# Attention maxima split on DVE before their transposition, copied out by ScalarE, and the output product moved ahead of it

## What is computed

```
q, k = rope(q), rope(k)                      # q = layernorm(x), k = v = context
Q, K, V = q @ Wq.T + bq, k @ Wk.T + bk, v @ Wv.T + bv      # 16 heads of 8
attn = softmax(Q K^T / sqrt(8)); out = (attn V) @ Wo.T + bo
x = x + tanh(g_xattn) * out
x = x + tanh(g_ffn) * ffn(layernorm(x))      # 8 experts of 352, top 2 of a router
```

## Time and profile before

| | us |
|---|---|
| median of 3 runs | 434.19 |
| lowest, highest | 433.54, 435.53 |
| the profiled execution, its own time | 435.61 |
| its span, first to last instruction | 433.8 |

### The profile page before, as it was taken

How to read it: one execution, slowest core, us unless ns; L and a number is a source line. 1 busy time by engine, 2 the same in 40 slices (tenths; PEclk the granted TensorE clock), 3 DMA queues, 4 the chain that set the end, 5 groups by cost and what they waited for, 6 DMA issues and landing times.

```text
span 433.8 us, 13431 instructions
## 1 busy us (share of the span) xinstructions
PE 391.3 (90%) x3876; PEld 267.6 (62%) x3877; DVE 302.5 (70%) x1167; ACT 260.1 (60%) x582; POOL 244.8 (56%) x201
## 2 busy tenths in 40 slices
PE   8997888999889888988998899998999999999991
PEld 3445454565656545555655578686777878778771
DVE  5878878898898978979786565568655555555550
ACT  3518577786967768676756665644455555454540
POOL 7073233135665555745343367888887458876663
PEclk9999999999999999999998999999999999999997
DMA  7525152353867914325101324544454334444320
GB/s 198 157 60 137 28 133 67 88 145 108 223 162 206 217 55 111 102 58 132 52 29 47 98 59 78 92 65 98 78 76 59 50 48 57 62 52 57 34 24 0
DMA packets 57423, 39.08 MB, mean 90 GB/s; under 512 B 8819, under 2 KB 55158, under 8 KB 57366
## 3 DMA queue, kind: packets, MB, share of 16 engines
q1 hardware_dynamic: 43622, 28.87, 26.1%
q0 software_dynamic: 12736, 8.64, 14.2%
q10 hardware_dynamic: 1008, 0.85, 0.8%
HBM read 14.26 MB, written 11.75 MB: 60 GB/s over the span
## 4 chain that ended last, share of the span: by engine, by line
PE 50%; DVE 17%; DMA 11%; issue 7%; SPq 6%; ACT 4%; POOLq 2%; POOL 1%; DVEq 0%; ACTq 0%
PE bank L1614 9%; PE bank L1592 7%; PE bank L1594 7%; DMA out<-ys,yi 5%; DVE nmx L847 5%; DMA ks<-parts 4%; PE bank L1604 4%; SPq L249 4%; PE bank L1374 3%; PE bank L1401 2%; PE bank L1348 2%; SPq L282 2%; PE bank L1316 2%; PE bank L1317 2%; ACT pt L580 2%
## 5 line engine op out<-in xcount | busy, mean ns | idle before, releaser
L516 POOL DMA_INDIRECT out<-ys,yi x72 | 111.8, 1553 | 43.5 <-issue 23.0
L427 POOL DMA_INDIRECT slots_dram<-xr,slu x64 | 65.5, 1024 | 75.0 <-ACT onT L593 55.1
L847 DVE TENSOR_REDUCE nmx<-bank 128x4 f32<-128x512 f32 x128 | 81.7, 680 | 4.3 <-PE bank L1348 4.3
L580 ACT ACTIVATE pt<-bank 128x512 f32<-128x512 f32 x128 | 72.5, 595 | 9.3 <-PE bank L1361 8.2
L1614 PEld LDWEIGHTS bank<-wf_sb,hT 128*128 128x128 f32 (+1 forms) x432 | 56.9, 190 | 22.7 <-issue 18.0
L1200 DVE TENSOR_TENSOR hh<-sg,bank 128x352 f32<-128x352 f32 x72 | 37.4, 520 | 47.9 <-ACT sg L714 27.2
L1614 PE MATMUL bank<-wf_sb,hT 128*128 (+1 forms) x432 | 61.0, 277 | 4.7 <-DVE hT L1210 4.6
L722 ACT ACTIVATE ys<-bank,yc 128x128 f32<-128x128 f32 x72 | 26.5, 368 | 64.0 <-PE bank L1614 60.1
L1592 PE MATMUL bank<-wf_sb,xT 128*128 x144 | 55.2, 465 | 0.1
L1594 PE MATMUL bank<-wf_sb,xT 128*128 x144 | 54.3, 459 | 0.0
L1374 PE MATMUL bank<-pt,v 128*9 128x128 f32 x1024 | 49.4, 276 | 3.7 <-ACT pt L580 2.5
(11 more groups left out here) (193 smaller groups left out, 707.9 us busy)
## 6 DMA issues: line engine op xcount, KB each, us to landing
qs<-parts SPq DMA_DIRECT2D x48, 128.0 KB
ks<-parts SPq DMA_DIRECT2D x45, 128.0 KB
xs<-slots_dram SPq DMA_DIRECT2D x72, 66.0 KB
wf_sb<-in_wup SPq DMA_DIRECT2D x8, 352.0 KB
x_sb<-in_x SPq DMA_DIRECT2D x8, 256.0 KB, 3.7
ctx_sb<-in_ctx_in SPq DMA_DIRECT2D x8, 256.0 KB, 4.5
out<-x_sb SPq DMA_DIRECT2D x8, 256.0 KB, 2.5
out<-ys,yi POOLq DMA_INDIRECT x72, 3.4
```

The source lines that it names most:

```text
L427: nc.gpsimd.indirect_dma_start(out=slots_dram, out_offset=bass.IndirectOffsetOnAxis(ap=slu[:, c % 2, k, kk:kk + 1], axis=0), in_=xr[:, c % ...
L516: nc.gpsimd.indirect_dma_start(out=out.rearrange("b s d -> (b s) d"), out_offset=bass.IndirectOffsetOnAxis(ap=yi[:, r:r + 1], axis=0), in_ ...
L580: nc.scalar.activation(pt[:, 4 * g:4 * g + 4, :], STB[g % 2][:, :].rearrange("p (h s) -> p h s", h=4), ACT.Exp, scale=SCORE_SCALE).then_in ...
L847: nc.vector.tensor_reduce(nmx[:, b % 2, at:at + 4], SB[g % 2][:, :].rearrange("p (h s) -> p h s", h=4), AX.X, ALU.max, negate=True).then_i ...
```

## The change

The maxima are split into two bf16 parts by DVE before the transposition (`split_high`, `split_low`, on 128 queries x 16 heads in SBUF). PE transposes both parts at once, 32 columns, by a bf16 product with the identity. ScalarE copies the result out of PSUM (`maximum_out`), behind `heads_out` of the next iteration. On PE the transposition moves behind `project_out`. SP, PE and POOL wait for the copy (`a_mT`) where they waited for L858. POOL's `low` gets a wait at u = 0 (for `choose_sum` of chunk c - 2) and at u = 3 (for the split of batch b + 2). Before the loop, the first remainder of chunk 1 moves behind the split of batch 1.

```diff
-        mTs = sb("mTs", [NH, 2, NMAX, S], BF16)
+        nm2 = sb("nm2", [128, 2, NMAX, NH], BF16)
+        mTs = sb("mTs", [NMAX * NH, 2, S], BF16)
-        mT_ps = SB[1][0:NH, 0:S]
+        mT_ps = SB[1][0:NMAX * NH, 0:S]
 ...
# SP, maxima
-                sp.wait_ge(d_mT, b + 1)
+                sp.wait_ge(a_mT, b + 1)
-                    sp.dma_start(qs[row:128:64, b // CH % NST, :, t0:t0 + S], mTs[:, b % 2, part, :])\
+                    sp.dma_start(qs[row:128:64, b // CH % NST, :, t0:t0 + S], mTs[NH * part:NH * (part + 1), b % 2, :])\
# POOL, scatter_early
-                pool.wait_ge(d_mT, min(b + 2, B))
+                pool.wait_ge(a_mT, min(b + 2, B))
# POOL, u == 0
                     if there(c + 1):
+                        if there(c - 2):
+                            pool.wait_ge(d_mb, c - 1)
                         low(c + 1, 1)
# POOL, u == 3
                     if there(c + 2):
+                        pool.wait_ge(d_ms, b + 3)
                         low(c + 2, 0)
# ScalarE
+            def maximum_out(b):
+                act.wait_ge(pe_mT, b + 1)
+                if b >= 2:
+                    act.wait_ge(m_in[b % 2], 32 * (b // 2))
+                nc.scalar.activation(mTs[:, b % 2, :], mT_ps, ACT.Copy).then_inc(a_mT, 1)
 ...
             high(1, 1, PR)
+            maximum_out(0)
             middle(1, 0)
+            maximum_out(1)
 ...
                 if real(b - 1):
                     heads_out(b - 1)
+                if b and real(b + 1):
+                    maximum_out(b + 1)
# DVE
-                if g == 0 and b >= 2:
-                    dve.wait_ge(pe_mT, b - 1)
 ...
-            def maximum_high(b):
-                dve.wait_ge(pe_mT, b + 1)
+            def split_high(b):
+                dve.wait_ge(d_max, 4 * b + 4)
                 if b >= 2:
-                    dve.wait_ge(m_in[b % 2], 32 * (b // 2))
-                nc.vector.tensor_copy(mTs[:, b % 2, 0, :], mT_ps).then_inc(d_mh, 1)
-
-            def maximum_low(b):
+                    dve.wait_ge(pe_mT, b - 1)
+                nc.vector.tensor_copy(nm2[:, b % 2, 0, :], nmx[:, b % 2, :]).then_inc(d_mh, 1)
+
+            def split_low(b):
                 dve.wait_ge(d_mh, b + 1)
-                nc.vector.tensor_tensor(mTs[:, b % 2, 1, :], mT_ps, mTs[:, b % 2, 0, :], ALU.subtract).then_inc(d_mT, 1)
+                nc.vector.tensor_tensor(nm2[:, b % 2, 1, :], nmx[:, b % 2, :], nm2[:, b % 2, 0, :], ALU.subtract).then_inc(d_ms, 1)
 ...
-            maximum_high(0)
-            maximum_low(0)
+            split_high(0)
+            split_low(0)
             for g in range(4):
                 maximum(1, g)
+            split_high(1)
+            split_low(1)
             remainder(1, 0, HB)
-            maximum_high(1)
-            maximum_low(1)
             remainder(1, 1, PR)
# PE
                 if g == 1 and b:
-                    pe.wait_ge(d_mT, b)
+                    pe.wait_ge(a_mT, b)
 ...
-                pe.wait_ge(d_max, 4 * b + 4)
-                nc.tensor.transpose(mT_ps, nmx[:, b % 2, :], ident).then_inc(pe_mT, 1)
+                pe.wait_ge(d_ms, b + 1)
+                mm(mT_ps, nm2[:, b % 2, :, :].rearrange("p a h -> p (a h)"), identb, start=True, stop=True).then_inc(pe_mT, 1)
 ...
+                if real(b - 1):
+                    project_out(b - 1)
                 if real(b + 2):
                     transpose_maximum(b + 2)
-                if real(b - 1):
-                    project_out(b - 1)
```

More of the change, by code:

```diff
@@ L193, in flamingo @@
         d_rq, d_rk, p_lq, p_lk, d_mh = map(sem, ("d_rq", "d_rk", "p_lq", "p_lk", "d_mh"))
+        d_ms, a_mT = sem("d_ms"), sem("a_mT")
         stack_in = [sem("stack_in0"), sem("stack_in1")]
@@ L200, in flamingo @@
             sem, ("a_tg", "a_xh", "a_xT", "a_exp", "a_aT", "a_xn", "a_nT", "a_e"))
-        d_max, d_mT, d_rc, d_on, d_x1, d_q = map(sem, ("d_max", "d_mT", "d_rc", "d_on", "d_x1", "d_q"))
+        d_max, d_rc, d_on, d_x1, d_q = map(sem, ("d_max", "d_rc", "d_on", "d_x1", "d_q"))
         d_stat, d_ve, d_rs, d_stat2, d_ve2, d_t2, d_sc2, d_rt, d_top, d_m12, d_slot, d_sl, d_pr = map(
@@ L1155, in _ @@
                 if real(b + 2):
-                    maximum_high(b + 2)
-                    maximum_low(b + 2)
+                    split_high(b + 2)
+                    split_low(b + 2)
                 if u == 1 and there(c + 2):
@@ L1499, in _ @@
                 keep_warm(STB[0], 1)
+            pe.wait_ge(cast, 1)
             transpose_maximum(0)
@@ L1504, in _ @@
             transpose_maximum(1)
-            pe.wait_ge(cast, 1)
             for b in range(B):
```

## The result

The changed kernel took 441.77 to 449.05 us in four runs, median 444.06, against 433.54 to 435.53 for the kernel before on the same chip. The ratio is 1.019 with an interval of 1.0135 to 1.024; on a second chip it was 1.021 (1.015 to 1.026). It is slower by about 2%: 434.19 times 1.019 is 442.4 us.

A forecast was written before the change was run, and what follows sets the result against it. The attention part was taken as paced by a round of all engines ahead of the maxima of u = 0, behind which SP's `ks` transfers stand. Delays over five chunks and the rest sum to 4.5 us: 438.7 us, range 431.5 to 442.5.

The forecast's parts named there:

- the two turns of ScalarE's queue: Turns u = 3 to 0 and 0 to 1: `oT` late behind `base` or `normalise`, copy behind it; 0.4 and 0.45 us.
- The operations: New or changed operations: split 0.19 us each, copy 0.28 with 0.18 of queue, L923 about 0.17, transposition 0.07 less.
- 2 us over 32 batches at most: PE's queue: the bf16 transposition takes about 0.05 us instead of 0.12, 0.07 less per batch.
- The turns: Four batch-to-batch turns of the chunk from 98.04: 0.25, 0.2, 0.4 and 0.45 us late, 1.3 in sum.
- ScalarE gets the copy, behind `heads_out`: ScalarE's queue: the copy starts 0.48 us after `oT` and takes 0.28; the second group of `scores` waits for it.
- 0.2 at u = 2: Turn u = 2 to 3: DVE does four statistics ahead of the split, so PE waits about 0.2 us for it.
- DVE's relief: DVE at u = 0: L923 freed from POOL's `low`, 3.4 us in five chunks; as rival it decides, faster, chance 0.2.
- The rival at 430.2 us: DVE's relief decides: L923's 3.4 us and the saved round trip come through, 4.0 us faster; chance 0.2.
- POOL holds the split: Rival at u = 0: POOL's `low` of k holds the split's subtraction, up to 1.2 us in five chunks, 444.7; chance 0.07.
- The wait costs nothing: POOL at u = 0: `low` of k, waiting for `choose_sum`, is done near 117.7, before SP wants it after 121.4.
- I count 0, with 1.5 us either way: Start, up to 45 us: first split makes maxima 0.1 us later, a `shift` may pass POOL sooner; counted as 0.
- 0.8, 0.6 and 0.1 us: Delays forecast for the chunk from 45.67, the chunk from 125.04 and everything from 180 us on.

The follow-up runs named there:

- the order alone: The output product put ahead of the transposition, nothing else changed, against the kernel before: 1.028 (1.023 to 1.0325).
- the kernel without products: The kernel before without the eight 128x512 products PE does between the first eight groups of scores, against the kernel before: 1.002 (0.998 to 1.006).

## Why the prediction was right, and where it was short

It forecast slower, 438.7 us within 431.5 to 442.5. The ratio makes 442.4, inside by 0.1 us and just outside the forecast's own 436 to 442; the median of the four runs as they stand is 444.06, above both. The change costs 8.2 us where the sum was 4.5. The direction and the two turns of ScalarE's queue were foreseen; that the size fell inside is luck. By its steps:

- **The operations.** Split 0.17 each (predicted 0.19), copy 0.25 with 0.15 of queue (0.28 and 0.18), L923 at 0.17: right. PE's transposition was to hold its queue 0.07 us less and holds it 0.04 more, and the stretch with the output product is 0.15 longer, 4.8 us over the kernel where "2 us over 32 batches at most" were to be won. This has the sign wrong.
- **The turns.** PE waits for the copy behind `oT` at u = 3 to 0 and u = 0 to 1, 0.96 to 0.97 and 0.55 us in each of chunks 2 to 5, and in chunk 1, which has no `base` yet, at u = 0 to 1 alone. For the split it waits 2.7 us in all, three times ahead of the first mark and once at u = 2 (0.54 us at 54.79); at u = 2 of the chunk shown it loses 0.06, and most of the 0.20 is PE's longer stretch. `heads_by_query` stands at 15.51 us from its chunk's first scores instead of 14.77, 0.74 late (predicted 0.8, as 0.25, 0.2 and 0.4; it is 0, 0.20 and 0.54), and SP is released by the copy, 1.13 us late. The chunks at full clock are longer by 3.20 us for 3.0. Right in the mechanism and in the total; that the terms add up so well is in part chance. At the clock of the kernel before the change costs 1.4% (0.7 to 2.0), 5.9 us, where the sum was 4.5.
- **Its cause.** "ScalarE gets the copy, behind `heads_out`" was told as the reason. The rows of the two turns bear it out. The experiments don't make it the whole: on DVE the copy was as late and the time 1.042, and with DVE's copy right behind the split, its waits gone, the time was still 1.017, for PE then waited for the split. Each way of splitting ahead of the transposition cost 1.7% or more, by one wait or another. The prediction priced the move of the output product at 0.07 us less and 0.2 at u = 2, and not the cover that the product had given, which the order alone on the kernel before shows to be worth something (1.028). How the loss divides into the copy's queue, this cover, PE's longer stretch and the clock, no run separates.
- **DVE's relief.** The rival at 430.2 us rested on L923. By itself the relief gives 0.999 (0.995 to 1.003), so nothing that can be measured: it was right to put it behind, and 0.2 was generous.
- **POOL holds the split.** The mechanism exists, for the low part of q rather than of k: 1.13 us on one subtraction. The change's own wait keeps it away. "The wait costs nothing" was right of the one for k on the kernel before, and the one for q seems to earn its place, by PE's waits more than by the time. What the prediction missed is that the low part released by it lands on L816.
- **The terms that fell short are "I count 0, with 1.5 us either way"** for the start, together with 0.8, 0.6 and 0.1 us for the chunks from 45.67 and 125.04 and for the rest. In the profile they are 2.43, 2.35, 1.73 and 3.79 us. Each was summed as if PE's products kept their durations, and in these stretches the clock fell. The start's 2.43 is above its bound of 1.5, but it is not in every execution: the same program up to there had 0.11 in the profile without POOL's waits. The profiled run has more of this than the others: of the 8.2 us by the ratio, products put into the waits gave back 0.6 to 0.7%, 2.6 to 3 us, not clear of noise.

## What to carry to other kernels

Before moving an operation to an idle engine, list the whole chain from its input to the one who waits, and beside it what the waiting engine has to do meanwhile; an order in which a product lay between request and use may be worth up to its duration, and a queue that looks free on average may hold the new operation behind just the work that is late. Price a moved or retyped product by the whole stretch of the queue around it, not by its own length: here 0.59 us became 0.74 and 0.79. A wait of TensorE near 1 us should be priced at its length, and as a risk at the products behind it that may run at half clock (three chunks with waits of 0.97, 0.55 and 0.77 us or so kept 1.00); products without use in the gap, in several profiles, test that. And a relief of an engine that is busy 66 to 70% of the time is worth nothing until the profile shows that something waits for it at that place.

## What the runs showed of the hardware

- The granted clock fell to its lower level behind short gaps of a TensorE that is 90% busy over the span: behind 0.97 and 0.25 us at the start of the changed kernel, behind 0.80, 0.45, 0.26 and 0.80 us in that of the kernel without products (0.50 for 12 us), behind 1.17 and 1.09 us in the loop. The gaps alone don't decide: the kernel before kept 1.00 behind 1.12 us at 36.78, and chunks 2, 3 and 5 of the changed kernel kept it with waits of 0.97, 0.55 and 0.77 us or so in each; without POOL's waits the same start kept it behind 0.97 and 0.25 us and fell only near 35 us, behind 0.88 and 0.79 more; and the start of the kernel before, in its profile with the wait for k, fell at 33.6 us behind 0.46, 0.46, 0.42 and 0.26. The Trainium skill's TensorE: Matmul & The Clock Gate, section "A second HAM failure mode: psum-queue depth-cycling", says that a TensorE that idles briefly and often between groups of products goes back and forth between the levels; these rows agree.
- Small DVE operations held beside one POOL operation of 1.16 us: a cast of 128x16 for up to 1.11 us instead of 0.17, a subtraction of 128x16 for up to 1.22 instead of 0.18, an addition of a constant to 128x4 for 0.85, which takes 0.16 on average in the kernel without POOL's two waits, and there L817 on 128x4 for up to 1.51, where it takes 0.10 in the changed kernel's chunk (L820 at 120.74).
- PE's stretch from the transposition or the fp32 output product, whichever comes first, over both and the bf16 bias to `scores_by_key`: 0.59 us with the fp32 transposition of 16 columns first, 0.74 with the bf16 one of 32 columns in either order, 0.79 with the fp32 one behind the output product, each in nearly every batch.
